# Two moves in one chain of layers: the third group's normalisation behind four query and key splits on VectorE, and the values' convolution of two groups ahead of sums and triangles on TensorE

## The chip, the cores and the metric

The kernel runs on one core of a Trainium2 chip. The metric is the device time of one execution in microseconds (us). The core has TensorE (PE, the matmuls), VectorE (DVE), ScalarE (ACT), GpSimd (POOL) and SyncE (SP, which only issues DMAs here). Each engine works through its own list of instructions in the order written; they meet only at semaphores.

## What is computed

Two layers on `x` of 2 x 1024 tokens with 128 features, with a layer normalisation behind each of four parts. Only the first and the third part matter here:

```python
x = _layernorm(x + _L0_attn_ref(x, ...))   # softmax attention, 8 heads
x = _layernorm(x + _L0_ffn_ref(x, ...))    # gated network, 512 hidden
x = _layernorm(x + _L1_attn_ref(x, ...))   # delta rule, 4 heads, chunks of 32
x = _layernorm(x + _L1_ffn_ref(x, ...))

# in _L0_attn_ref
xn = (x - mu) * rsqrt(var + eps) * gamma + beta
q, k, v = xn @ Wq + bq, xn @ Wk + bk, xn @ Wv + bv
p = softmax(q @ k.T / sqrt(dk))

# in _L1_attn_ref
q = silu(causal_dwconv(x @ Wq, conv_q))    # the same for k and v
q, k = l2norm(q), l2norm(k)
A = kb @ k.T                               # per head and chunk of 32
T = inv(eye + tril(A, -1))
```

## The kernel before, in words

The order of work is written out by hand: one program per engine, with a semaphore wait wherever one engine needs another's result. The tokens are cut into four groups of 512 (`GROUPS`, numbered 0 to 3 here; "the third group" is group 2).

**The first stage** makes the queries, keys and values of the first attention. For a group `g`, DVE takes statistics (`x_stats(g)`), POOL raises them to the power -0.5 (`x_rstd(g)`, line 903), and DVE writes the normalised rows (`normalise_x(g)`, line 1199, four instructions of 128x128). PE transposes them (`xn_transposes(g)`, line 1751), ACT copies them out with gamma and beta (`load_xnT(g)`, line 660), and PE multiplies with the three weights (`project_q`, `project_k`, `project_v`, lines 1760, 1767, 1780). Queries and keys are wanted in two parts: ACT writes the leading one (`leading_q`, `leading_k`, lines 666 and 670), and DVE the rest (`rest_q`, `rest_k`, lines 1205 and 1210). SP stores both parts to scratch in DRAM (lines 385 to 392), first of all the 32 rows that heads 0 and 1 need, of groups 0 and 1, in eight DMAs; when all eight have landed (`first_rows_stored`), SP and ACT load head 0's stacks `qst` and `kst` (lines 409, 410, 683, 684). PE's first row scores (`row_scores`, lines 1806 and 1807) wait for these, and DVE takes the row maxima (`row_max`, line 1245). On PE the row scores stand behind `project_v(2)`, and that group's own products behind `project_v(1)`, which waits for `values(0)` on DVE (line 1222). `values(0)` waits for `bv_spread`, a copy that ACT makes right behind `load_xnT(2)` (line 681). After that come 32 half heads of scores, exponentials (line 703) and products, each with a small transfer of its negated row maxima into the stack (`load_shift`, line 415).

**The third stage**, about 349 to 412 us into the span, makes the queries, keys and values of the delta rule. For each group PE does three convolutions, `conv(g, i)` with `i` 0 for the keys, 1 for the queries and 2 for the values (12 matmuls each, lines 1679 to 1681), the gates (`gate_products`, line 1689), the transposes of the next group's input (`transposes`, line 1664), the sums of squares of keys and queries (`sums(g, 0)` and `sums(g, 1)`, line 1699), and for the group before it the values' and keys' transposes (`v_to_tokens`, line 1710, `k_to_tokens`, line 1720) and the products within chunks (`triangles`, 256 small matmuls, line 1740). ACT applies silu to each convolution (line 730), copies the transposes (`vtok_copy`, line 635, `ktok_copy`, line 639), loads the next group's input (`load_x`, lines 620 and 622), and then changes its table, takes the gates' exponentials and the inverse norms (`norms`, lines 629 and 631), and changes the table back. DVE splits the loaded input (`split_x`, line 1129), squares (`square`, line 1137), scales by the norms (`normalise`, line 1142), makes the gates' logits (lines 1150 to 1160) and masks the triangles (lines 1179 and 1180). In group 0 it also finishes the normalisation of the layer before (`normalise_rows2(3)`, line 1103), while POOL prepares filters (lines 1023 to 1027). The keys' and the values' convolution of one group use the same bank, so the second waits for the silu of the first. Behind this stage stand the inverses of the triangles, one batch on POOL and one on DVE (`invert`, lines 549 and 551), a long row of filter matmuls (line 1917), the recurrence and the last network.

The list of PE in the third stage, which the change edits:

```python
for g in range(GROUPS - 1):
    conv(g, 0)
    gate_products(g)
    ...
    transposes(g + 1)
    conv(g, 1)
    ...
    if g >= 1:
        v_to_tokens(g - 1)
    sums(g, 0)
    if g >= 1:
        triangles(g - 1)
    conv(g, 2)
    if g >= 1:
        k_to_tokens(g - 1)
    sums(g, 1)
```

Of the kernel before, what the change touches and what calls it, by code (L numbers as in the profile page):

```python
# [56 lines left out]
def program(nc, dr, out_dram, x_dram, q_scratch, k_scratch, ctx):  # L57
# [201 lines left out]
    def nth_conv(g, i):  # L259
        return 3 * g + KQV_ORDER[g].index(i) + 1  # L260

    def nth_norm(g, i):
        return 2 * g + (i if g < GROUPS - 1 else 1 - i) + 1
# [3 lines left out]
    with nc.Block() as block:  # L267
# [818 lines left out]
        def _(dve):  # L1086
# [97 lines left out]
            def x_stats(g):  # L1184
                dve.wait_ge(x_in[g], 16)
                for n in range(4):
                    last = nc.vector.bn_stats(st6[:, g, n, :], X[:, 4 * g + n, :])
                link(last)
                for n in range(4):
                    last = nc.vector.bn_aggr(mv[:, g, n, :], st6[:, g, n, :])  # L1190
                link(last)
                nc.vector.tensor_scalar(rs[:, g, :], mv[:, g, :, 1], LN_EPS, None, ALU.add).then_inc(x_stats_ready, 1)

            def normalise_x(g):
                dve.wait_ge(x_rstd_ready, g + 1)
                if g >= 2:
                    dve.wait_ge(xnT_psum, g - 1)
                for n in range(4):
                    last = nc.vector.tensor_scalar(xn[:, g % 2, n, :], X[:, 4 * g + n, :], mv[:, g, n, 0:1],
                                                   rs[:, g, n:n + 1], ALU.subtract, ALU.mult)  # L1200
                last.then_inc(xn_ready, 1)

            def rest_q(g):
                dve.wait_ge(q_hi, g + 1)
                nc.vector.scalar_tensor_tensor(qsp[g][:, 1, :], ps[:, Q_BANK[g], :], bq[:, 0:1], qsp[g][:, 0, :].bitcast(F32),
                                               ALU.add, ALU.subtract).then_inc(q_lo, 1)

            def rest_k(g):
                dve.wait_ge(k_hi, g + 1)
                nc.vector.scalar_tensor_tensor(ksp[g][:, 1, :], ps[:, K_BANK[g], :], bk[:, 0:1], ksp[g][:, 0, :].bitcast(F32),  # L1210
                                               ALU.add, ALU.subtract).then_inc(k_lo, 1)
# [3 lines left out]
            normalise_x(0)  # L1215
            normalise_x(1)
            x_stats(2)
            normalise_x(2)
            def values(g):
                b, half = g // 2, g % 2  # L1220
                dve.wait_ge(v_psum, g + 1)
                nc.vector.tensor_tensor(vp[:, 8 * b:8 * b + 8, 4 * half:4 * half + 4, 0:DK0],
                                        ps[:, V_BANK, :].rearrange("p (t h e) -> p h t e", t=4, e=DK0),
                                        bv_all[:].rearrange("p (h o e) -> p h o e", o=1, e=DK0).broadcast_to([P, 8, 4, DK0]), ALU.add).then_inc(v_ready, 1)
# [3 lines left out]
            rest_k(0)  # L1228
            rest_q(1)
            rest_k(1)  # L1230
            x_stats(3)
            dve.wait_ge(bv_spread, 1)
            values(0)
# [351 lines left out]
        def _(pe):  # L1585
# [58 lines left out]
            def y_product(g):  # L1644
                pe.wait_ge(lo2_ready, 12 * g + 12)
                for k in range(FB):
                    last = product3(ps[:, 7, :], weights(W3 + D * k, D), (h2_hi[:, 2, k, :], h2_lo[:, 2, k, :]), k == 0, k == FB - 1)
                last.then_inc(y2_psum, 1)
# [18 lines left out]
            def conv(g, i):  # L1667

                if i != 1 and i == KQV_ORDER[g][0] and g >= 1:
                    pe.wait_ge(silu_done, 3 * g)  # L1670
                if i == 1 and g >= 1:
                    pe.wait_ge(ln_done, 2 * g)
                if i == KQV_ORDER[g][2]:
                    pe.wait_ge(silu_done, 3 * g + 1)
                bank = ps[:, (1, 2, 1)[i], :]
                for t in range(CONV):
                    cols = slice(GT * (g % 2) + t, GT * (g % 2) + t + GT)
                    xh, xl = x_hi[:, g // 2, cols], x_lo[:, g // 2, cols]
                    nc.tensor.matmul(bank, wc_lo[:, i, t, :], xh, start=(t == 0), stop=False)  # L1679
                    nc.tensor.matmul(bank, wc_hi[:, i, t, :], xl, start=False, stop=False)  # L1680
                    last = nc.tensor.matmul(bank, wc_hi[:, i, t, :], xh, start=False, stop=(t == CONV - 1))
                last.then_inc(conv_psum, 1)

            def gate_products(g):
                pe.wait_ge(xf_ready, g + 1)
                if g >= 1:
                    pe.wait_ge(ln_done, 2 * g - 1)
                for n in range(4):
                    last = nc.tensor.matmul(ps[:, 3, 20 * n:20 * n + 20], xf[:, P * n:P * n + P], wgates[:], start=True, stop=True)
                last.then_inc(gates_psum, 1)  # L1690

            def sums(g, i):

                pe.wait_ge(sq_ready, nth_norm(g, i))
                if i == 0:
                    pe.wait_ge(gates_biased, g + 1)
                else:
                    pe.wait_ge(silu_done, 3 * g + 2)
                nc.tensor.matmul(ps[:, (3, 2)[i], :], head_ones[:], sq[:, i, :], start=True, stop=True).then_inc(ss_psum, 1)

            def v_to_tokens(g):
                pe.wait_ge(silu_done, nth_conv(g, 2))
                for loaded in (xf_ready, xhi_ready, xlo_ready):
                    pe.wait_ge(loaded, min(g + 3, GROUPS))
                if g == GROUPS - 1:
                    pe.wait_ge(ktok_ready, g)
                for n in range(4):
                    t = 4 * g + n
                    off = FIRL - 1 + P * (t % 8)
                    last = nc.tensor.transpose(ps[:, 0, P * n:P * n + P], vpad[:, t // 8, off:off + P], ident[:])  # L1710
                last.then_inc(vtok_psum, 1)
# [216 lines left out]
            for g in range(GROUPS - 1):  # L1928
                pe.wait_ge(xhi_ready, g + 1)
                pe.wait_ge(xlo_ready, g + 1)  # L1930
                conv(g, 0)
                gate_products(g)
                if g == 0:
                    y_product(GROUPS - 1)
                transposes(g + 1)
                conv(g, 1)
                if g == 0:
                    y2_to_tokens(GROUPS - 1)
                if g >= 1:
                    v_to_tokens(g - 1)  # L1940
                sums(g, 0)
                if g >= 1:
                    triangles(g - 1)
                conv(g, 2)
                if g >= 1:
                    k_to_tokens(g - 1)
                sums(g, 1)
# [297 lines left out]
```

## Time and profile before

| what | before |
|---|---|
| median of 3 runs | 593.5 us (591.52 to 593.85) |
| the profiled execution, its own time | 589.53 us |
| its span in the trace | 587.8 us |
| PE busy | 545.9 us, 93% |
| DVE busy | 398.1 us, 68% |
| ACT busy | 325.6 us, 55% |
| POOL busy | 178.7 us, 30% |
| mean granted TensorE clock | 0.988 |

Times of an instruction are its start from the span's beginning and its duration. "Busy" leaves out waiting. The chain of waits is the row of pieces that ended last, followed back from the last instruction; what isn't on it costs nothing as long as it stays off it. A granted clock of 1.00 is 2.4 GHz, 0.50 is 1.2 GHz.

### The profile page before, as it was taken

To read this page: it belongs to the slowest core of one execution; us is meant where nothing else is said; L and a number is where in the kernel's file an instruction comes from. 1 tells how busy PE (TensorE), PEld (TensorE's weight loads), DVE (VectorE), ACT (ScalarE), POOL (GpSimd) and SP (SyncE) were. 2 spreads that over 40 slices of the span, in tenths; PEclk is the share of its full clock that TensorE was granted. 3 is DMA by queue.
4 is the path that set the end of the run, shared out by engine and by line. 5 is a ranking of instruction groups with operands and counts; after the bars stand their busy time and mean duration, and the time that the engine had idled before them with its cause. 6 is when DMAs were issued, how large, how long until landed. Compare 5 with 4: busy or idle time off the path is not lost.

```text
span 587.8 us, 17528 instructions
## 1 busy us (share of the span) xinstructions
PE 545.9 (93%) x7486; PEld 372.9 (63%) x7486; DVE 398.1 (68%) x766; ACT 325.6 (55%) x575; POOL 178.7 (30%) x343
## 2 busy tenths in 40 slices
PE   3699999999999999999999999799999789989995
PEld 2445555555555556777778787577566677667774
DVE  5697999998999945354452534444889961379685
ACT  2317888788888885656556554367832430125441
POOL 7100111353554433010010103428987225010202
PEclk9899999999999999999999999899999989999998
DMA  4688756555332000001000000012374300000001
GB/s 121 140 233 211 211 130 148 108 124 97 73 58 57 3 4 2 0 1 38 1 1 1 1 1 0 10 29 44 61 127 103 75 4 3 5 3 1 0 20 54
DMA packets 54227, 33.82 MB, mean 58 GB/s; under 512 B 39029, under 2 KB 45685, under 8 KB 54150
## 3 DMA queue, kind: packets, MB, share of 16 engines
q1 hardware_dynamic: 48998, 31.65, 24.0%
q10 hardware_dynamic: 5152, 1.05, 1.1%
q8 instruction: 59, 0.97, 0.7%
q14 instruction: 18, 0.15, 0.1%
HBM read 20.83 MB, written 9.44 MB: 51 GB/s over the span
## 4 chain that ended last, share of the span: by engine, by line
PE 68%; DVE 12%; DMA 8%; ACT 6%; issue 3%; SPq 1%; POOL 1%; POOLq 0%; ACTq 0%; DVEq 0%
PE ps L1842 10%; PE ps L1827 9%; PE ps L1589 7%; PE ps L1590 7%; PE ps L1591 7%; DMA qst<-shift_sb 5%; PE ps L2027 3%; DVE inv_flat L549 3%; PE ps L2159 3%; PE ps L1806 3%; PE ps L2160 3%; DVE inv_flat L551 2%; ACT prob L703 2%; PE ps L2019 2%; PE ps L1679 1%
## 5 line engine op out<-in xcount | busy, mean ns | idle before, releaser
L1245 DVE TENSOR_REDUCE nmx<-ps 128x1 f32<-128x1024 f32 x128 | 154.1, 1217 | 16.5 <-PE ps L1807 15.2
L703 ACT ACTIVATE prob<-ps 128x512 f32<-128x512 f32 x256 | 137.5, 597 | 26.3 <-PE ps L1827 26.0
L1842 PE MATMUL ps<-prob,vp 128*32 128x128 f32 x2048 | 78.9, 278 | 0.0
L1827 PE MATMUL ps<-qst,kst 50*128 50x512 f32 x256 | 73.5, 492 | 4.5 <-ACT prob L703 3.4
L1842 PEld LDWEIGHTS ps<-prob,vp 128*32 128x32 f32 x2048 | 49.1, 109 | 39.7 <-ACT prob L703 22.7
L1118 DVE TENSOR_TENSOR h_lo<-hf,h_hi 128x512 fp32r<-128x512 f32 x48 | 33.1, 689 | 52.4 <-ACT h_hi L607 50.2
L1589 PE MATMUL ps<-h_hi,w_lo 128*128 128x512 f32 x144 | 57.9, 402 | 2.4 <-DVE h_lo L1118 2.4
L1590 PE MATMUL ps<-h_lo,w_hi 128*128 128x512 f32 x144 | 57.0, 396 | 0.0
L1591 PE MATMUL ps<-h_hi,w_hi 128*128 128x512 f32 x144 | 56.9, 395 | 0.0
L1806 PE MATMUL ps<-kst,qst 48*128 48x512 f32 x128 | 52.7, 413 | 2.3 <-DMA kst<-k_scratch 1.7
L1807 PE MATMUL ps<-kst,qst 48*128 48x512 f32 x128 | 51.4, 403 | 0.0
L1827 PEld LDWEIGHTS ps<-qst,kst 50*128 50x128 f32 x256 | 29.3, 183 | 34.5 <-ACT prob L703 22.9
L606 ACT ACTIVATE hf<-ps,ffn_scale 128x512 f32<-128x512 f32 x32 | 22.1, 691 | 34.3 <-PE ps L1591 32.7
L885 POOL TENSOR_SCALAR rs<-mv 128x4 f32<-128x4 f32 x8 | 3.0, 376 | 122.4 <-DVE mv L1096 122.3
L924 POOL CAST nsplit<-nmx 128x4 fp32r<-128x4 f32 x32 | 6.0, 188 | 105.3 <-DVE nmx L1245 103.0
L1917 PE MATMUL ps<-vpad,fir_diag 32*32 32x512 f32 x1088 | 36.7, 597 | 0.1
L1589 PEld LDWEIGHTS ps<-h_hi,w_lo 128*128 128x128 f32 x144 | 27.0, 188 | 11.8 <-issue 4.0
L1591 PEld LDWEIGHTS ps<-h_hi,w_hi 128*128 128x128 f32 x144 | 27.0, 188 | 6.5
L1590 PEld LDWEIGHTS ps<-h_lo,w_hi 128*128 128x128 f32 x144 | 27.1, 188 | 6.0
L837 ACT ACTIVATE h_hi<-ps 128x512 fp32r<-128x512 f32 x32 | 17.7, 601 | 22.4 <-PE ps L2160 19.8
L1917 PEld LDWEIGHTS ps<-vpad,fir_diag 32*32 32x32 f32 x1088 | 21.3, 103 | 13.2 <-issue 6.3
L1806 PEld LDWEIGHTS ps<-kst,qst 48*128 48x128 f32 x128 | 23.7, 185 | 6.4 <-DVE nmx L1245 3.7
(262 smaller groups left out, 1101.5 us busy)
## 6 DMA issues: line engine op xcount, KB each, us to landing
qst<-q_scratch SPq DMA_DIRECT2D x31, 192.0 KB, 4.5
kst<-k_scratch SPq DMA_DIRECT2D x31, 192.0 KB, 5.0
w_raw<-L_ffn_h_w SPq DMA_DIRECT2D x8, 256.0 KB, 3.9
kd<-ka SPq DMA_DIRECT2D x8, 256.0 KB, 6.0
X<-L_attn_x SPq DMA_DIRECT2D x4, 256.0 KB, 5.3
qst<-shift_sb SPq DMA_DIRECT2D x64, 4.0 KB
q_scratch<-w_hi SPq DMA_DIRECT2D x2, 512.0 KB, 5.2
k_scratch<-w_lo SPq DMA_DIRECT2D x2, 512.0 KB, 3.2
```

Source lines behind the costliest of these rows:

```text
L606: nc.scalar.activation(hf[:, o, :], bank, ACT.Gelu, scale=scale)
L703: nc.scalar.activation(prob[:, n % PROBS, GT * (t % 2):GT * (t % 2) + GT], ps[:, RINGB + i % RING, :], ACT.Exp, scale=SCORE_SCALE).then_in ...
L1118: nc.vector.tensor_tensor(h2_lo[:, layer, o, :], hf[:, o, :], h2_hi[:, layer, o, :].bitcast(F32), ALU.subtract).then_inc(lo2_ready, 1)
L1245: nc.vector.tensor_reduce(nmx[:, u % 2, j:j + 1], pair, AX.X, ALU.max, negate=True).then_inc(max_done, 1)
L1589: nc.tensor.matmul(out, wl, xh, start=start, stop=False)
L1590: nc.tensor.matmul(out, wh, xl, start=False, stop=False)
L1591: return nc.tensor.matmul(out, wh, xh, start=False, stop=stop)
L1806: nc.tensor.matmul(ps[:, bank, :], qst[0:48, p, P * k:P * k + P], kst[0:48, p, 0:GT], start=True, stop=True)
L1807: nc.tensor.matmul(ps[:, bank + 1, :], qst[64:112, p, P * k:P * k + P], kst[64:112, p, GT:S], start=True, stop=True).then_inc(max_psum, 1)
L1827: nc.tensor.matmul(ps[:, RINGB + i % RING, :], kst[r:r + 50, p, P * t:P * t + P], half_of(qst[r:r + 50, p, :], u % 2), start=True, stop=Tr ...
L1842: last = nc.tensor.matmul(ps[32 * j:32 * j + 32, PVB, P * half:P * half + P], vp[:, h, t, :], prob[:, n % PROBS, c:c + P], start=(t == 0), ...
L1917: last = nc.tensor.matmul(ps[32 * g:32 * g + 32, FIR_BANK[k] + h, :], fir_diag[f, (0, FIRL)[k] + t, :], vpad[f, g // 2, off:off + GT], sta ...
```

## The change

Nothing is added or removed. On DVE the four instructions of `normalise_x(2)` move behind `rest_q(0)`, `rest_k(0)`, `rest_q(1)` and `rest_k(1)`, ahead of `x_stats(3)`. On PE `conv(g, 2)` of groups 0 and 1 moves ahead of `sums(g, 0)` (and for group 1 of `triangles(0)` too); of group 2 it stays where it is.

```diff
@@ DVE, first stage
             normalise_x(0)
             normalise_x(1)
             x_stats(2)
-            normalise_x(2)
...
             dve.wait_ge(qk_bias_in, 2 * 16)
             rest_q(0)
             rest_k(0)
             rest_q(1)
             rest_k(1)
+            normalise_x(2)
             x_stats(3)
             dve.wait_ge(bv_spread, 1)
             values(0)
@@ PE, third stage
                 if g >= 1:
                     v_to_tokens(g - 1)
+                if g < 2:
+                    conv(g, 2)
                 sums(g, 0)
                 if g >= 1:
                     triangles(g - 1)
-                conv(g, 2)
+                if g == 2:
+                    conv(g, 2)
                 if g >= 1:
                     k_to_tokens(g - 1)
                 sums(g, 1)
```

The order on DVE in the first stage, as a difference. Names in brackets are semaphores; `rstd_ready` is POOL's power, `q_hi` and `k_hi` are the leading parts from ACT.

```order
-L1199 TENSOR_SCALAR xn<-X,mv,rs 128x128 [waits xnT_psum,rstd_ready]
-L1199 TENSOR_SCALAR xn<-X,mv,rs 128x128 x3
 L1205 SCALAR_TENSOR_TENSOR qsp<-ps,bq,qsp 128x512 [waits q_hi,qk_bias_in]
 L1210 SCALAR_TENSOR_TENSOR ksp<-ps,bk,ksp 128x512 [waits k_hi]
 L1205 SCALAR_TENSOR_TENSOR qsp<-ps,bq,qsp 128x512 [waits q_hi]
 L1210 SCALAR_TENSOR_TENSOR ksp<-ps,bk,ksp 128x512 [waits k_hi]
+L1199 TENSOR_SCALAR xn<-X,mv,rs 128x128 [waits xnT_psum,rstd_ready]
+L1199 TENSOR_SCALAR xn<-X,mv,rs 128x128 x3
```

The four rests no longer stand behind the normalisation and its wait for POOL.

The order on PE in the third stage, group 1, before. Semaphores of the first stage are used again here, so the names in brackets are old ones: `stats_ready` is that a square is ready, `bv_spread` that the gates' logits are, `bv_summed` counts the silus. L1710 is `v_to_tokens(0)`, L1699 `sums`, L1740 `triangles(0)`, L1679 the first matmul of a convolution, L1720 `k_to_tokens(0)`.

```order
L1710 MATMUL ps<-ident,vpad 128x128 [waits wv_in,qk_bias_in,qk_weights_in,bv_summed]
L1710 MATMUL ps<-ident,vpad 128x128 x3
L1699 MATMUL ps<-sq,head_ones 128x512 [waits bv_spread,stats_ready]
L1740 MATMUL ps<-kq 32x64 [waits xnT_ready]
L1740 MATMUL ps<-kq 32x64 x63
L1679 MATMUL ps<-x_hi,wc_parts 128x512 [waits bv_summed]
...
L1720 MATMUL ps<-ident,kq 128x128 [waits q_psum,xnT_ready]
```

The same place of the changed kernel, where every line number is one higher:

```order
L1711 MATMUL ps<-ident,vpad 128x128 [waits wv_in,qk_bias_in,qk_weights_in,bv_summed]
L1711 MATMUL ps<-ident,vpad 128x128 x3
L1680 MATMUL ps<-x_hi,wc_parts 128x512 [waits bv_summed]
...
L1700 MATMUL ps<-sq,head_ones 128x512 [waits bv_spread,stats_ready]
L1741 MATMUL ps<-kq 32x64 [waits xnT_ready]
L1741 MATMUL ps<-kq 32x64 x63
L1721 MATMUL ps<-ident,kq 128x128 [waits q_psum,xnT_ready]
```

The twelve matmuls of the values' convolution now stand between the transposes and the wait for the square.

## Rows read from the trace of the kernel before

**Rows 1.** The page, the chain that ended last, shares by line.

```profile
PE ps L1842 10%; PE ps L1827 9%; PE ps L1589 7%; PE ps L1590 7%; PE ps L1591 7%; DMA qst<-shift_sb 5%; PE ps L2027 3%; DVE inv_flat L549 3%; PE ps L2159 3%; PE ps L1806 3%; PE ps L2160 3%; DVE inv_flat L551 2%; ACT prob L703 2%; PE ps L2019 2%; PE ps L1679 1%
```

**Rows 2.** The chain in order of time (start, duration, what), first stage and attention.

```profile
16.85 0.35 SPq L385
...
20.05 2.02 DMA k_scratch<-ksp
...
22.50 5.75 DMA kst<-k_scratch
...
28.92 1.23 DVE nmx L1245
...
44.84 5.56 DMA qst<-shift_sb
...
112.78 4.07 DMA qst<-shift_sb
```

**Rows 3.** Timeline, first stage: start, duration, engine, line, operation [idle before <-releaser].

```profile
13.27 0.69 ACT L666 ACTIVATE qsp<-ps,bq 128x512 fp32r<-128x512 f32 x1 [1.17 <-PE ps L1760]
13.45 2.71 DVE L1199 TENSOR_SCALAR xn<-X,mv,rs 128x128 f32<-128x128 f32 x4 [1.49 <-POOL rs L903]
...
16.26 0.69 ACT L670 ACTIVATE ksp<-ps,bk 128x512 fp32r<-128x512 f32 x1 [0.17 <-PE ps L1767]
...
17.45 0.66 PE L1751 MATMUL ps<-ident,xn 128*128 128x128 f32 x4
...
18.07 0.73 DVE L1210 SCALAR_TENSOR_TENSOR ksp<-ps,bk,ksp 128x512 fp32r<-128x512 f32 x1
...
18.83 0.25 ACT L681 COPY bv_all<-ps 128x128 f32<-128x128 f32 x1
...
20.11 0.69 DVE L1222 TENSOR_TENSOR vp<-ps,bv_all 128x512 f32<-128x512 f32 x1
...
20.85 2.08 PE L1780 MATMUL ps<-wv_sum,xnT 128*128 128x128 f32 x8 [2.74 <-DVE vp L1222]
...
25.63 1.06 PE L1780 MATMUL ps<-wv_sum,xnT 128*128 128x128 f32 x8
```

**Rows 4.** Stretches: bounds, length, busy of PE, PEld, DVE, ACT, POOL, PEclk, DMA.

```profile
22.00:23.00 1.00, 1.00 (x6) 1.00 (x5) 0.47 (x3) 0.00 (x0) 0.00 (x0) 0.50 0.00 0
...
370.50:374.60 4.10, 0.84 (x5) 0.42 (x4) 3.95 (x16) 1.20 (x3) 0.94 (x3) 1.00 0.00 0
374.60:377.60 3.00, 2.94 (x131) 2.00 (x131) 0.61 (x2) 0.00 (x0) 0.00 (x0) 0.70 0.02 5
```

**Rows 5.** The chain in order of time, third stage, groups 0 and 1.

```profile
359.20 0.86 PE ps L1699 x2
...
362.89 0.60 ACT vpad L730
...
370.55 0.69 DVE x_lo L1129
...
373.94 0.68 DVE sq L1137
...
377.62 0.73 PE ps L1679
...
381.40 0.47 ACT vpad L730
...
381.89 0.58 ACT ka L639
```

**Rows 6.** Timeline, third stage: POOL and DVE side by side, and triangles of group 2.

```profile
368.14 2.38 POOL L1023 TENSOR_TENSOR fir_diag<-eye,fir_l 128x992 f32<-128x992 f32 x1
...
370.82 0.62 POOL L1027 TENSOR_SCALAR wo<-wo,rmsw 128x128 f32<-128x128 f32 x1
...
371.15 1.11 DVE L1103 TENSOR_SCALAR X<-X,mv,rs 128x128 f32<-128x128 f32 x4
...
404.50 1.48 PE L1740 MATMUL ps<-kq 32*32 32x64 f32 x128
```

## The prediction

> **What bounds the kernel now.** I read the page first. Its chain of waits is spread over all stages [rows 1]: the attention's matmuls, the gated network's, the inverses on DVE, the last network. No engine bounds everything, so an edit pays only where the chain passes it. I then read the chain in order of time around both edits, the timeline there for the instructions that the chain leaves out, and the busy time of short stretches for the clock.
>
> In the first stage the chain runs from DVE to SP [rows 2]: the first store of a split query starts at 16.85, eight stores follow one another, the last one lands at 22.07, the loads of head 0's stacks land at 28.25, and only then does DVE take its first row maximum (28.92). The reader is to see what stands ahead of 16.85. The leading part of group 0's queries was ready at 13.27 + 0.69 = 13.96 [rows 3], and DVE could have made the rest then, but it was at 13.45 inside `normalise_x(2)`, which took 2.71 us.
>
> In the third stage the chain passes PE's `sums(0, 0)`, then ACT's silu of the values at 362.89, a long run of ACT, the split of the input at 370.55 and the square of group 1 at 373.94, `sums(1, 0)` right behind it, and only at 377.62 the values' convolution of group 1 [rows 5]. Between 370.50 and 374.60 PE is busy for 0.84 us of 4.10, and in the next 3.00 us its granted clock is 0.70, that is, partly at 1.2 GHz; before it fell PE had idled for 3.3 of those 4.1 us, waiting for the split and the square [rows 4]. The convolution needed nothing of what it stood behind.
>
> **The change, part one: the third group's normalisation.** The four rests now follow ACT. `rest_q(0)` can start at 14.0 in place of 16.1. `rest_k(1)` waits for the leading part that ACT ends at 16.26 + 0.69 = 16.95, so with its 0.73 us it ends at 17.7 in place of 18.8 [rows 3]. On SP the first store goes out at 14.8; eight issues of some 0.46 us each would be through by 18.4, but the last two need `rest_k(1)`: they go out at 17.9 and 18.3, where the last went out at 20.05 [rows 2]. The stacks' loads start 1.7 us earlier on SP. Of head 0's four loads two are issued by ACT, behind the copy of `bv_spread`, and that gets later, as follows.
>
> The moved normalisation starts at 17.75 and takes 1.11 us, the price of the same four instructions where POOL is mostly done [rows 6]; it ends at 18.9. PE's transposes of that group start then in place of 17.45. From their start to the end of the bias copy ACT and PE took 18.83 + 0.25 - 17.45 = 1.63 us [rows 3], so that copy ends at 20.6 in place of 19.08. `values(0)` started at 20.11, held by the statistics of the fourth group on DVE; these took the 1.3 us between 18.80 and 20.11 and end at 20.2 now, so the copy becomes its release: 20.65 to 21.35. `project_v(1)` starts at about 21.45 in place of 20.85. PE's block from there to the end of `project_v(2)` took 25.63 + 1.06 - 20.85 = 5.84 us, over half of it at 1.2 GHz [rows 3, 4], and ends at 27.3. ACT's loads go out at 20.7 and 21.1 in place of the 22.09 and 22.50 that released the chain, and land at 21.1 + 5.75 = 26.85. The row scores start with the later of the two, at 27.3; before, they started just behind the landing at 28.25, some half a microsecond ahead of the row maximum at 28.92 [rows 2], at 28.4. That is a gain of 1.1 us. Bounds: 0, if the loads land no earlier, since they share the queues with what follows; 1.6, if PE keeps its 2.4 GHz through the shorter idle (1.9 us in place of 2.74, broken by the transposes) and the landing is what ends last. I take 1.1, the sum of the rows as they stand. From the first row maximum on, DVE and PE are busy one behind the other, so it passes on.
>
> **Part two: the values' convolution.** Group 0: `sums(0, 0)` costs the chain 0.86 us between the transposes and the convolution [rows 5]. The convolution moves ahead of it, and its silu starts at 362.0 in place of 362.89. Both sums are done by 362.86 + 0.86 = 363.7 as before, before ACT reads them, so they are now hidden beside ACT's table load. ACT runs without an outside wait from there to the copies that feed the split of group 2's input; the split starts at 369.7 in place of 370.55. PE ends `conv(1, 1)` at 370.5 as before, since its total work is unchanged.
>
> Group 1: the values' transposes start at 370.55, the convolution at 371.0, and at full clock it takes 362.89 - 360.06 = 2.83 us [rows 5], so it ends at 373.8. The square ended at 373.94 + 0.68 = 374.62; 0.86 earlier it ends at 373.76. So the convolution fills the wait exactly, PE has next to no idle time, and the clock should stay at 2.4 GHz. Then `sums(1, 0)` 0.86, `triangles(0)` 1.41 to 1.48, the price of the same 128 recorded matmuls in group 2 at full clock [rows 6], and `k_to_tokens(0)` 0.66, as four transposes took at 17.45 [rows 3]: ACT's copy of the keys starts at 376.8 in place of 381.89. That is 5.1 us, made of 0.86 of `sums(0, 0)`, some 2.8 of the convolution that moved into the idle time, and some 1.4 that the same work took longer at 1.2 GHz (377.62 to 381.40 for the convolution alone, against 2.83 [rows 5]). ACT's table load follows that copy in both orders, and from there each wait is relative: the same pieces at the same distances, up to the inverses on DVE.
>
> Against this stands one contact that is new. `normalise_rows2(3)` follows the split on DVE and ran at 371.15, when POOL had 0.3 us left of its last filter instruction [rows 6]. It now starts at 370.4, beside the end of the first and the whole of the last two of POOL's three. The nearest row is `normalise_x(2)` at 13.45, the same kind of instruction beside POOL's head sums: 2.71 us for four that cost 1.11 elsewhere, 1.6 us too long [rows 3]. POOL is through at 371.44 here, so at most 371.44 - 370.4 = 1.0 us of standing still can come, and none at least; square, sums and all behind would be that much later. I take 0.4, since the four instructions can slip in between POOL's, as the fact that 13.45's four did not wait for all of POOL's work suggests. The Trainium skill (SBUF — State Buffer, section "Who interferes with whom") states that a DVE instruction in a two-port mode and GpSimd exclude each other for a whole instruction, whoever comes second waiting; by that rule the delay is nearer 1.0 than 0.4, and it speaks against this half of the change. The row at 13.45 agrees with it.
>
> Part two gives 5.1 - 0.4 = 4.7 us, with 3.6 and 5.2 as ends.
>
> **The sum.** 1.1 + 4.7 = 5.8 us. The profiled execution took 589.53 us, so the changed one would take 583.7. The median of the runs lies 4.0 us above that execution (593.5), so the forecast of the median is 593.5 - 5.8 = **587.7 us**.
>
> **The rivals.**
> *The start gives nothing.* The loads are limited by what the queues move, or PE's block gets later than I sum. For it: PE's block ends within 0.5 us of the landing. Against it: the first store is 2 us earlier and SP issued without a gap. Only part two stays: 593.5 - 4.7 = 588.8.
> *POOL and DVE collide in full.* By the row at 13.45 the four instructions lose 1.6 us, and POOL's own end is pushed back with them: part two gives 5.2 - 1.6 = 3.6, the whole 4.7, the time 588.8. By the skill's rule named above this is the case to expect wherever both run; the trace so far has it at one place out of the two that I looked at.
> *The gain of part two is eaten later.* Behind the third stage stand two inverses on two engines, some 25 us of filter matmuls and transfers. If one of them is held by something that did not move, the rest waits for it. Against it: all of them start from results of this stage. I price it at half of part two: 593.5 - 1.1 - 2.3 = 590.1, and up to 592.
> *Slower: the attention falls into another phase.* The shift transfers stand on the chain in six places, with landings from 4.07 to 5.56 us [rows 2]. A shift may land late when the large loads of later stacks are under way. The start of scores moves by 1.1 us against transfers that move by 1.7. If all six took the longest landing in place of about 4.3, this adds up to 7 us, and 593.5 - 5.8 + 7 = 594.7. It decides from an added landing of about 1 us at every place. Against it: every load of the attention waits for a score or an exponential, so the transfers move along. That the change doesn't do what it says is ruled out by the two orders shown ahead.
>
> **How the numbers follow.** The forecast gets 0.60, the start without gain 0.14, the full collision 0.12, the eaten gain 0.10, the slower case 0.04. The forecast's own range is 586.0 to 589.0. Runs of the kernel before differ by 2.3 us among three, so the range of 8 in 10 reaches from 585.3 to 591.0: it takes in the two rivals at 588.8 and half of the eaten case. About 0.5%, 3 us, is what a measurement can tell from no change. Faster by more means below 590.5: 0.60 + 0.14 + 0.12 and a little of the eaten case, less some for the spread of runs, 0.87. Within 0.5%: 0.10. Slower: 0.03.
>
> **What would show it.** In the profile of the changed kernel: the first store's issue near 14.8, the last of the eight near 18.3, the first row maximum at 27.8 or so; granted clock between 21 and 24 us tells which end part one has. In the third stage: the values' silu of group 0 near 362.0 less what part one gave; no idle time of PE over 0.7 us ahead of `sums(1, 0)`; a granted clock of 1.00 through group 1; `normalise_rows2(3)` between 1.1 and 2.1 us long; the keys' copy 4.7 us closer to the start of the stage. The forecast is wrong if PE still idles 2 us ahead of that sum, if DVE's squares get later than the convolution's end by over 1 us, or if the distance from the keys' copy to the end has grown.

## The result and the profile after

| | median of the runs, us | lowest to highest | runs | profiled execution, its span, us |
|---|---|---|---|---|
| kernel before | 592.51 | 588.71 to 593.85 | 4 (the three shown ahead and a fourth, 588.71) | 589.53, 587.8 |
| changed kernel | 584.21 | 583.73 to 584.70 | 4 | 584.60, 582.8 |

The ratio is 0.987, with a 95% interval of 0.9821 to 0.992: the kernel became faster, by more than was forecast. 584.2 lies 3.5 us below the forecast of 587.7 and 1.1 us below the low end of its range (585.3). Between the two profiled executions the difference is 4.9 us, and the interval reaches from 4.7 to 10.6 us, so the first question is how large the gain is at all. A few runs of nearly every kernel are over 1.5% longer than its fastest one; medians and ranges here include them, the ratios leave them out.

**The page.** The groups that stood at the head of the chain are still there, with lines one to four further down in the code [rows 1]. From the page of the changed kernel:

```profile
span 582.8 us, 17528 instructions
PE 546.2 (94%) x7486; PEld 372.8 (64%) x7486; DVE 395.0 (68%) x766; ACT 325.5 (56%) x575; POOL 177.9 (31%) x343
PEclk9799999999999999999999999999999889999998
PE 76%; DVE 12%; ACT 5%; DMA 4%; issue 2%; SPq 1%; POOL 0%; POOLq 0%; DVEq 0%; ACTq 0%
```

**First stage.** The timeline of the changed kernel (start, duration, engine, line, operation, and in brackets the idle time before and its releaser), to be held against [rows 3]:

```profile
14.57 0.35 SPq L385 DMA_DIRECT2D q_scratch<-qsp  x1
...
16.21 0.75 DVE L1210 SCALAR_TENSOR_TENSOR ksp<-ps,bk,ksp 128x512 fp32r<-128x512 f32 x1
...
16.88 1.11 DVE L1199 TENSOR_SCALAR xn<-X,mv,rs 128x128 f32<-128x128 f32 x4
...
17.79 0.43 SPq L392 DMA_DIRECT2D k_scratch<-ksp  x1
...
19.42 0.26 ACT L681 COPY bv_all<-ps 128x128 f32<-128x128 f32 x1
...
20.22 0.45 ACTq L684 DMA_DIRECT2D kst<-k_scratch  x1
20.45 1.78 PEld L1781 LDWEIGHTS ps<-wv_sum,xnT 128*128 128x128 f32 x8 [1.99 <-DVE vp L1222]
20.45 2.08 PE L1781 MATMUL ps<-wv_sum,xnT 128*128 128x128 f32 x8 [1.75 <-DVE vp L1222]
...
27.39 0.50 PE L1807 MATMUL ps<-kst,qst 48*128 48x512 f32 x1
...
27.93 1.22 DVE L1246 TENSOR_REDUCE nmx<-ps 128x1 f32<-128x1024 f32 x1 [0.48 <-PE ps L1808]
```

The stores go out 2.3 us earlier, the moved normalisation takes 1.11 us in place of 2.71, and the first row maximum comes at 27.93 in place of 28.92 [rows 2]. What held the row scores is no longer the landing of the stacks: PE runs without a pause from 20.45 to them, at 1.2 GHz for most of that time. The busy time of three stretches of the changed kernel (bounds, length, PE, PEld, DVE, ACT, POOL, granted clock, DMA share, GB/s):

```profile
17.00:21.00 4.00, 1.21 (x6) 0.97 (x7) 3.50 (x16) 0.93 (x2) 1.01 (x1) 0.80 0.59 134
21.00:25.00 4.00, 4.00 (x12) 2.45 (x11) 1.32 (x5) 0.69 (x1) 0.00 (x0) 0.50 1.01 238
25.00:27.00 2.00, 2.00 (x12) 1.38 (x11) 1.04 (x2) 1.02 (x2) 0.00 (x0) 0.70 1.01 170
```

A granted clock of 0.80 over 4 us means 4 x 0.20 x 2 = 1.6 us at half clock; with the other two that makes 1.6 + 4.0 + 1.2 = 6.8 us. The clock fell between 19.30 and 19.40, over a microsecond before PE had work again (20.45):

```profile
17.00:19.30 2.30, 0.66 (x4) 0.42 (x4) 2.23 (x13) 0.56 (x1) 0.00 (x0) 1.00 0.86 200
19.40:20.40 1.00, 0.00 (x0) 0.00 (x0) 0.69 (x1) 0.27 (x2) 0.94 (x1) 0.50 0.00 0
```

In the 2.3 us before the fall PE had been busy for 0.66, the group's transposes. In the kernel before it fell at 20.8, as PE's block began (20.85), and stayed down for 3.4 us. The two profiles differ earlier too, where their code is the same. The first product of the keys, in the kernel before and in the changed one:

```profile
12.96 1.54 PE L1767 MATMUL ps<-xnT,wk 128*128 128x512 f32 x2
12.72 1.02 PE L1768 MATMUL ps<-xnT,wk 128*128 128x512 f32 x2
```

At 12.7 us PE was already at its quick pace in the changed kernel, and in the first profile only at about 14.0. That isn't work of the edit, and it comes up again below.

**Third stage.** The timeline of the changed kernel around group 1:

```profile
368.40 0.69 DVE L1129 TENSOR_TENSOR x_lo<-ps,x_hi 128x512 fp32r<-128x512 f32 x1 [3.42 <-ACT x_hi L622]
...
369.00 0.62 POOL L1027 TENSOR_SCALAR wo<-wo,rmsw 128x128 f32<-128x128 f32 x1
369.00 1.20 DVE L1103 TENSOR_SCALAR X<-X,mv,rs 128x128 f32<-128x128 f32 x4
...
371.87 1.28 DVE L1137 TENSOR_TENSOR sq<-kq 128x512 f32<-128x512 f32 x2
...
372.28 0.39 PE L1682 MATMUL ps<-x_hi,wc_parts 128*128 128x512 f32 x1
...
372.61 1.12 PE L1700 MATMUL ps<-sq,head_ones 128*128 128x512 f32 x2
372.71 0.60 ACT L730 ACTIVATE vpad<-ps 128x512 f32<-128x512 f32 x1 [2.22 <-PE ps L1682]
373.67 1.48 PE L1741 MATMUL ps<-kq 32*32 32x64 f32 x128
...
375.82 0.58 ACT L639 COPY ka<-ps 128x512 f32<-128x512 f32 x1 [2.51 <-PE ps L1721]
```

and the stretch around it:

```profile
370.00:376.00 6.00, 6.00 (x147) 4.07 (x146) 3.80 (x14) 1.27 (x3) 0.00 (x0) 1.00 0.01 3
```

The last matmul of the values' convolution (372.28) runs into the sums of the squares (372.61): PE is busy for all 6 us, and the granted clock is 1.00 where it was 0.70 [rows 4]. The keys' copy starts at 375.82 in place of 381.89 [rows 5], 6.07 us earlier. Of these 1.29 had been gained before this stage (its first input split starts that much earlier); 4.78 are gained in it.

**Behind it.** The end moved by 4.9 us, not by 6.07. The chain of the changed kernel in order of time (start, duration, what), at the second inverse:

```profile
415.77 0.51 SPq L494
416.28 0.04 issue
416.32 3.89 DMA low_dram<-low
420.21 0.02 issue
420.23 3.88 DMA inv_flat<-low_dram
424.11 0.02 issue
424.13 0.22 DVE inv_flat L549
```

and of the kernel before:

```profile
421.75 0.51 SPq L494
422.26 0.04 issue
422.30 1.91 DMA low_dram<-low
424.21 0.02 issue
424.22 3.72 DMA inv_flat<-low_dram
427.94 0.02 issue
427.97 0.67 DVE inv_flat L549
```

The store leaves 5.98 us earlier, but lands after 3.89 us in place of 1.91; the inverse starts only 3.84 us earlier. Behind it PE ran at half clock twice near 460 and 467 (3.4 us each), where before it did so once, near 471.

### The profile page after: what moved, and what is told of

It reads as the page before. It is cut to its first block, busy times and chain, and to the rows that moved or that the text cites. A ratio compares the mean times of both kernels' runs of the same rounds, so it can differ in the third digit from the quotient of the medians.

```text
span 582.8 us, 17528 instructions
## 1 busy us (share of the span) xinstructions
PE 546.2 (94%) x7486; PEld 372.8 (64%) x7486; DVE 395.0 (68%) x766; ACT 325.5 (56%) x575; POOL 177.9 (31%) x343
## 4 chain that ended last, share of the span: by engine, by line
PE 76%; DVE 12%; ACT 5%; DMA 4%; issue 2%; SPq 1%; POOL 0%; POOLq 0%; DVEq 0%; ACTq 0%
PE ps L1843 11%; PE ps L1828 10%; PE ps L1590 7%; PE ps L1592 7%; PE ps L1591 7%; PE ps L2031 3%; DVE inv_flat L549 3%; PE ps L1807 3%; PE ps L2163 3%; PE ps L2164 3%; DVE inv_flat L551 2%; ACT prob L703 2%; DMA qst<-shift_sb 2%; PE ps L2023 2%; PE ps L1680 2%
## 5 line engine op out<-in xcount | busy, mean ns | idle before, releaser
L1246 DVE TENSOR_REDUCE nmx<-ps 128x1 f32<-128x1024 f32 x128 | 154.0, 1217 | 14.7 <-PE ps L1808 13.4
L1918 PEld LDWEIGHTS ps<-vpad,fir_diag 32*32 32x32 f32 x1088 | 21.0, 103 | 13.5 <-issue 6.6
L2163 PE MATMUL ps<-h_lo,wc_parts 128*128 128x512 f32 x64 | 26.8, 419 | 0.9 <-DVE h_lo L1472 0.9
```

The costliest lines, as they stand in the source:

```text
L1246: nc.vector.tensor_reduce(nmx[:, u % 2, j:j + 1], pair, AX.X, ALU.max, negate=True).then_inc(max_done, 1)
L1918: last = nc.tensor.matmul(ps[32 * g:32 * g + 32, FIR_BANK[k] + h, :], fir_diag[f, (0, FIRL)[k] + t, :], vpad[f, g // 2, off:off + GT], sta ...
L2163: nc.tensor.matmul(ps[:, 4 + o, :], w, h_lo[:, 0, k, :], start=(k == 0), stop=False)
```

## The experiments

Eleven experiments ran, with nine different kernels, on three chips: 1 to 4 on the first, 5 to 8 on the second, 9 to 11 on the third. On each the kernel before ran beside them: medians 589.78 (32 runs), 589.82 (26) and 589.4 (17). Numbers of lines in brackets below are those of the kernel before, unless said otherwise.

**1. The kernel before, unchanged.** No edit.

> The kernel before, unchanged, to see how far its executions lie apart. Theory A (the forecast's sum of 6 us holds, and the other 2 to 3 us of the measured 8.3 are the spread of the kernel before): its runs scatter again over 588 to 594 us, and this profile differs from the first at a place that can be named, a cold stretch of TensorE or a late landing. Theory B (the sum is too small by 2 us in a typical run, and the first profile of the kernel before was untypically quick): nearly all runs lie at 591 to 594 and the profile shows where 2 to 4 us more go than in the first one.

Measured: 590.36 us (588.78 to 594.31, 12 runs), ratio 1.0006 (0.9981 to 1.003). With the runs beside it there are 87 of this kernel, with the median 589.8; 11 of them took 593.5 us or more. So the profiled execution of 589.53 us was a typical one, and the median of three from which the forecast started (593.5) was a high one: theory A. At a rate of 11 in 87, two of three runs at 593.5 or more come about once in 20 times. Chance is therefore the likely reason, not a shown one; on which chip the first comparison ran is not on record.

**2. The start alone.**

```
             x_stats(2)
-            normalise_x(2)
...
             rest_k(1)
+            normalise_x(2)
             x_stats(3)
```

> Only the third group's normalisation is moved. Forecast's theory: 1.1 us faster (0 to 1.6), first row maximum about 27.9 us into the span. Rival: nothing at all at the end, as the attention settles to its own pace. If the first stage is where the kernel before scatters, this kernel's runs lie closer together and its median gains more than 1.1 us.

Measured: 590.56 us (587.55 to 592.8, 12 runs), ratio 1.0001 (0.9974 to 1.0027). No gain shows in the times; the interval leaves room for 1.5 us, so it decides neither for the forecast nor for its rival. In this profile the first row maximum stood at 28.03, where experiment 1 had it too. What its run shows besides is the price of group 1's wait. The stretch 368 to 382, in experiment 1 and in experiment 2 (columns as above):

```profile
368.00:382.00 14.00, 10.68 (x162) 7.05 (x161) 5.97 (x19) 4.24 (x9) 5.80 (x12) 0.88 0.07 10
```

```profile
368.00:382.00 14.00, 10.68 (x159) 7.28 (x158) 5.85 (x18) 3.10 (x6) 5.33 (x11) 0.76 0.06 11
```

14 x 0.24 x 2 = 6.7 us at half clock against 14 x 0.12 x 2 = 3.4, with the same order of instructions and the same idle time on PE. From the split of group 2's input [L1129] to the gates of group 1 [L1167] this execution took 14.83 us, against 13.63 in the first profile and 13.67 in experiment 1.

**3. The convolutions alone.** Groups 0 and 1, the start as before.

```
+                if g < 2:
+                    conv(g, 2)
                 sums(g, 0)
...
-                conv(g, 2)
+                if not (g < 2):
+                    conv(g, 2)
```

> Only the values' convolution of groups 0 and 1 is moved. Forecast's theory: 4.7 us faster (3.6 to 5.2), no idle time of PE over 0.7 us ahead of the sum of group 1. Theory B puts the missing 2 us here: 6 to 7 us faster in the median, since the idle stretch that goes costs more at 1.2 GHz in most runs than in the one profiled.

Measured: 586.03 us (584.87 to 594.74, 9 runs), ratio 0.9928 (0.9898 to 0.9958), that is 4.2 us with the interval 2.5 to 6.0. No half clock in group 1, and PE doesn't idle ahead of `sums(1, 0)`; from L1129 to L1167 10.16 us. The interval holds the forecast of 4.7 and leaves out theory B's 6 to 7.

**4. The changed kernel again.**

> Both moves, again. If the parts add up, its gain is that of the two kernels with one part each, and lies between 5 and 8.5 us; its runs stay within 1.5 us of each other as in the first measurement.

Measured: 585.88 us (582.91 to 595.04, 12 runs), ratio 0.9918 (0.9883 to 0.9953): 4.8 us against the kernel before on the same chip. From the split to the gates 9.67 us, first row maximum at 27.50. Two things expected here did not come: the gain is just under the 5 to 8.5 us, and the runs don't lie within 1.5 us of each other.

**5. Group 1's convolution alone.**

```
+                if g == 1:
+                    conv(g, 2)
                 sums(g, 0)
...
-                conv(g, 2)
+                if not (g == 1):
+                    conv(g, 2)
```

> Of the three moves only the values' convolution of group 1 goes ahead; group 0 and the first stage are as before. Theory: the square of group 1 is ready 0.86 us later than with both groups moved, so PE idles about 0.8 us behind the convolution; from the split of group 2's input on DVE (the start of L1129) to the gates' sigmoids of group 1 (L1167) the distance of 13.6 us shrinks by 3.9 us, and no stretch of group 1 runs at 1.2 GHz. Rival: the distance shrinks by all 4.8 us, and group 0's move is worth nothing. In the median 3 to 4 us faster than before.

Measured: 585.54 us (584.17 to 589.42, 9 runs), ratio 0.9933 (0.9911 to 0.9956). From L1129 to L1167 9.57 us, 4.06 fewer than before, at a granted clock of 1.00. The 0.8 us of idle time that I expected behind the convolution isn't there: PE started the convolution at 372.76 and was busy until the sums at 375.66. One instruction block in one iteration carries nearly all of what part two gains.

**6. Only the clock.** The kernel before, with eight matmuls ahead of `sums(1, 0)` whose results nothing reads, in a bank that is free there.

```
+                if g == 1:
+                    for _ in range(8):
+                        nc.tensor.matmul(ps[:, 7, :], wc_hi[:, 0, 0, :], x_hi[:, 0, 0:GT], start=True, stop=True)
                 sums(g, 0)
```

> The kernel before with eight extra matmuls (results unused) in the idle time of PE ahead of the sum of group 1: only the clock is kept, no work is moved. Theory: the clock's share of part two is 1.4 us when the stretch at 1.2 GHz is 3.4 us long and more when it is 6.8 us long, so the distance from L1129 of group 2's input to L1167 of group 1 shrinks by 1.2 to 1.6 us against the first profile, and the median by 1 to 2 us. Rival: the clock is a bystander, nothing changes, and all of part two is the work moved into the idle time.

Measured: 587.87 us (585.25 to 599.58, 12 runs), ratio 0.997 (0.9948 to 0.9992), that is 1.8 us with the interval 0.5 to 3.1. The convolution still stands behind the sums; only the waiting time is filled. The timeline of this kernel, and its stretch:

```profile
373.77 1.29 DVE L1137 TENSOR_TENSOR sq<-kq 128x512 f32<-128x512 f32 x2
374.51 1.12 PE L1699 MATMUL ps<-sq,head_ones 128*128 128x512 f32 x2 [0.79 <-DVE sq L1137]
375.57 1.48 PE L1740 MATMUL ps<-kq 32*32 32x64 f32 x128
376.97 0.50 PE L1679 MATMUL ps<-x_hi,wc_parts 128*128 128x512 f32 x1
```

```profile
368.00:382.00 14.00, 12.53 (x176) 8.97 (x175) 6.51 (x20) 5.43 (x9) 6.99 (x14) 1.00 0.09 15
```

In experiment 2 the same sums took 2.08 us and the triangles 1.89 on the chain, both at half clock; here the timeline has 1.12 and 1.48. From L1129 to L1167 it is 12.47 us, 1.16 fewer than before. So the filled wait is worth 1.2 us at one half-clock stretch of 3.4 us, 2.4 at one of 6.8, and the moved work makes the rest of the 4.06.

**7. A filled wait in the first stage.** The changed kernel, with eight matmuls without a reader ahead of `project_v(1)`.

```
+            pe.wait_ge(q_hi, 1)
+            pe.wait_ge(k_hi, 1)
+            for _ in range(8):
+                nc.tensor.matmul(ps[:, 5, :], ksp[0][:, 0, 0:P], qsp[0][:, 0, :], start=True, stop=True)
             project_v(1)
```

> The changed kernel with eight extra matmuls (results unused) in PE's idle time between the third group's transposes and project_v(1). Theory: in the changed kernel PE's block at 1.2 GHz, not the landing of head 0's stacks, is what the first row scores wait for; with the clock kept the block ends 1.5 us earlier, the landing decides, and the first row maximum comes at 26.6 to 27.2 us in place of 27.5 to 27.9. Rival: the landing is as late as the block, nothing is gained, or the fill itself delays project_v(1). Median 0 to 1 us below that of the changed kernel.

Measured: 582.6 us (581.43 to 584.25, 6 runs), ratio 0.9881 (0.9857 to 0.9905). The timeline of its PE, with its own line numbers (L1796 is the fill, L1781 `project_v`, L1811 the row scores):

```profile
18.71 2.08 PE L1796 MATMUL ps<-qsp,ksp 128*128 128x512 f32 x8
20.71 1.16 PE L1781 MATMUL ps<-wv_sum,xnT 128*128 128x128 f32 x8
...
26.50 0.46 PE L1811 MATMUL ps<-kst,qst 48*128 48x512 f32 x1 [1.58 <-DMA kst<-k_scratch]
```

and its stretch:

```profile
16.00:28.00 12.00, 9.13 (x50) 6.16 (x48) 8.44 (x24) 3.41 (x6) 1.01 (x1) 1.00 0.86 181
```

The eight matmuls of `project_v(1)` take 1.16 us in place of 2.08, PE is through by 24.9, and the landing of the stacks ends last: the row maximum moves to 27.03, 0.9 us ahead of the changed kernel's first profile. The median lies 2.3 us below the 584.9 of all runs of the changed kernel, more than the 0 to 1 us expected, but no run of the changed kernel stood beside it on this chip.

**8. All three convolutions ahead of the sums.**

```
-                if g < 2:
+                if True:
                     conv(g, 2)
...
-                if g == 2:
+                if not (True):
                     conv(g, 2)
```

> The changed kernel with group 2's values' convolution moved ahead as well. Theory: PE idles only 0.84 us there, so the move hides at most that; the triangles of group 1 come some 2 us later and with them POOL's inverse, while the keys' copy on ACT stays within 0.5 us of where it was: same time as the changed kernel, or up to 1 us slower. Rival: the 4 us gain of group 1 repeats itself, 2 us or more faster.

Measured: 584.95 us (582.43 to 589.18, 12 runs), ratio 0.9927 (0.9905 to 0.9949). That is no gain over the changed kernel in the times, as expected. In the trace group 2's distance from the split [L1129] to the gates [L1167] is 9.51 us against 9.76 in the changed kernel's first profile, so 0.25 us and not 4.

**9. The same with a longer fill near the end.** Experiment 7, and nineteen filling matmuls in place of the eight that the kernel already issues ahead of `times_inverse(1)`.

```
-            keep_busy(7, 8)
+            keep_busy(7, 19)
```

> The changed kernel with the eight extra matmuls in the first stage and, behind the first batch's state inputs, 19 idle-time matmuls in place of 8, so that PE has next to no idle time ahead of the second batch's times_inverse (L1988 in the changed kernel), which took 5.50 us at 1.2 GHz against 3.95 us at full clock. Theory: the half-clock stretch goes, the 128 recorded matmuls take 3.95 us, and the median is 1 to 1.5 us below that of the kernel with the first fill alone. Rival: the added 11 matmuls (some 2.4 us at full clock) outlast the landing of the inverse and cost what they save: no difference.

Measured: 585.35 us (580.64 to 591.73, 12 runs), ratio 0.9907 (0.987 to 0.9943). Its profile shows no half clock there (1.00 from 455 to 475), but the times gain nothing: on the same chip the shorter fill had 583.81 (experiment 10). The fill ends at 465.15 and `times_inverse(1)` starts at 465.07, where the shorter fill let it start at 464.25 in experiment 10. Against that delay of 0.8 us stand 1.55 where the 128 recorded matmuls take 5.50 us, at half clock for the most part (experiment 4), and next to nothing where they take 4.14 or 3.95 without the longer fill (experiments 10 and 11). The half clock that this fill was to remove isn't there in every execution.

**10. Experiment 7 again.** Same kernel.

> The changed kernel with the eight extra matmuls in the first stage alone, again, beside the changed kernel on the same chip. Theory: 0.3 to 1.5 us below the changed kernel in the median; the first row maximum at 27.0 against 27.5 to 27.9 us. Rival: the 3 us between the two medians measured on two chips so far were chance, no difference.

Measured: 583.81 us (582.03 to 585.16, 6 runs), ratio 0.9898 (0.9857 to 0.994), first row maximum at 27.17, granted clock 1.00 in the first stage. That is 0.7 us below the changed kernel on the same chip (experiment 11).

**11. The changed kernel, a third time.**

> The changed kernel a third time, on the same chip as the two fills. By the forecast's sum, taken from the kernel before's own median of all runs (589.8 us), 584.0 us; by the first ratio (0.987) 582.1; by the second (0.9918) 585.0.

Measured: 584.51 us (581.32 to 597.64, 6 runs), ratio 0.9894 (0.985 to 0.9938). All 22 runs of the changed kernel have the median 584.9, the 12 of experiments 7 and 10 have 583.3. The fill of the first stage is the best version that ran, but the intervals overlap, and experiment 9, which has the same fill, had 585.35: a gain of 0.7 to 1.6 us over the changed kernel is likely and not settled. Experiment 11 itself fell between the 584.0 of the forecast's sum and the 585.0 of the second ratio.

## Why the prediction was wrong, and where it was right

Four places of the program separate the terms. The traces give, in us (the row maximum and the start of the third stage, the third of the four instructions of group 3's statistics [L1096], as starts; the others as distances):

| execution | first row maximum | start of third stage | from there to group 1's gates | from the gates to the end |
|---|---|---|---|---|
| before | 28.92 | 361.51 | 22.67 | 203.6 |
| experiment 1 (before) | 28.03 | 360.82 | 22.70 | 203.5 |
| experiment 2 (start alone) | 28.03 | 360.46 | 23.87 | 203.9 |
| experiment 3 (convolutions alone) | 28.88 | 361.66 | 18.34 | 204.0 |
| changed kernel | 27.93 | 360.22 | 17.89 | 204.7 |
| experiment 4 (changed kernel) | 27.50 | 359.96 | 17.85 | 205.7 |
| experiment 11 (changed kernel) | 27.64 | 360.02 | 18.15 | 201.4 |

**The terms of the sum were right, part one in the traces alone.** Part one was forecast at 1.1 us. The five executions with the start as before (the first profile and experiments 1, 3, 5, 6) have their first row maximum at 28.82 on average, the five with the moved normalisation (changed kernel, 2, 4, 8, 11) at 27.75: 1.1 us. At the start of the third stage the same two sets are 1.5 us apart. The medians of experiments 1 and 2 do not show this part.

In the changed kernel's first profile the number came out by two errors of a microsecond that cancelled. I had left ACT's leading part of the keys at 16.26 [rows 3]; it came at 15.49, since PE had reached its quick pace earlier in this execution, so the bias copy ended at 19.68 and not 20.6, and PE's block began at 20.45 and not 21.45. And the block took 26.40 + 1.06 - 20.45 = 7.0 us, not the 5.84 of before, with 6.8 us at half clock where the first profile had 3.4. Where PE reached that pace as late as in the first profile, in experiments 2, 4 and 8, the steps came as forecast:

| | forecast | exp. 2 | exp. 4 | exp. 8 |
|---|---|---|---|---|
| first store goes out | 14.8 | 14.54 | 15.02 | 15.00 |
| last of the eight goes out | 18.3 | 18.29 | 18.42 | 18.52 |
| bias copy ends | 20.6 | 20.47 | 20.59 | 20.69 |
| PE's block begins | 21.45 | 21.25 | 21.37 | 21.47 |
| PE's block ends | 27.3 | 27.07 | 27.03 | 27.19 |
| stacks land (ACT's second load) | 26.85 | 27.35 | 26.77 | 26.68 |
| row scores start | 27.3 | 27.49 | 26.96 | 27.12 |

In experiments 4 and 8 PE's block ended last, as forecast, in experiment 2 the landing.

So the size of part one depends on that draw. With the late pace the row maximum stands at 29.01 (the first profile, 3, 5, 6) against 27.73 (2, 4, 8): 1.3 us. With the early pace it is 28.03 (experiment 1) against 27.79 (changed kernel, 11): 0.2 us, from three executions only. With the half clock filled away it is 27.03 on average (7, 9, 10), so the half clock costs the changed order some 0.7 us.

Part two was forecast at 4.7 us and measured 4.78 at the keys' copy; by the table's third column it is 4.8 in the changed kernel and experiment 4, 4.5 in experiment 11 and 4.3 in experiment 3, against the mean of 22.67 and 22.70. Of its own terms, the 0.86 of `sums(0, 0)` came out exactly (values' silu 360.74 against 362.89: 2.15 = 1.29 + 0.86), the clock 1.2 us at one stretch of 3.4 us (experiment 6) against 1.4, the convolution 2.9 (experiment 5 less experiment 6) against 2.8. The forecast gives part two's whole once as 5.1 and once as 5.2, and its bounds add up to 586.7 to 589.9, not to 586.0 to 589.0; nothing hangs on either.

**The contact on DVE was over-priced.** I took 0.4 us for `normalise_rows2(3)` beside POOL, with 0 and 1.0 as bounds. It took 1.20 us against 1.11: 0.1, and the same 1.20 or 1.21 in all eight profiles with group 0's convolution moved. It did run beside the end of one filter instruction (368.67 + 0.35) and all of the last (369.00, 0.62). POOL was through at 369.62, so by the rule of the Trainium skill (SBUF — State Buffer, section "Who interferes with whom") the first of the four should have been held until then, some 0.6 us; it took 0.44 in place of 0.34, and the POOL instruction its usual 0.62. Here the measurement speaks against the rule for these pieces. So does the first profile: the first of the four started at 371.15 and took 0.37 us, though the same POOL instruction ran from 370.82 to 371.44. The four at 13.45 had agreed with it: they took 1.28, 0.76, 0.57 and 0.33 us, and the first three ended within 0.1 us of the POOL instruction beside them. Why one pair collides and the other doesn't is left open.

**The step that failed is the last one: the base.** "The median of the runs lies 4.0 us above that execution (593.5), so the forecast of the median is 593.5 - 5.8." The sum from the profiled execution, 583.7, was 0.5 us from the 584.2 measured in four runs. I then added the whole distance between the median of three runs and that execution, as if it were an overhead that every run has. It was not: with 87 runs the median of the kernel before is 589.8, and 11 of 87 lie at or above 593.5. From 589.8 the same sum gives 584.0, against 584.9 measured over 22 runs. For the same reason the gain of the first comparison, 8.3 us between medians, is too large. The ratios of experiments 4 and 11 stand for 4.8 us (2.8 to 6.9) and 6.2 us (3.7 to 8.8) of 589.8; the two medians over all runs lie 4.9 us apart, as do the two profiled executions. The sum of 5.8 is within both intervals, and up to a microsecond above these differences.

**Where that microsecond can go.** "The gain of part two is eaten later" was priced at half of part two, with the inverses held by something that did not move. Nothing of the kind holds them: in experiments 4 and 11 the inverse on DVE starts at 421.63 and 421.74, 6.3 and 6.2 us earlier than before. In the first profile the store of 3.89 us took 2.0 us of it and part was regained; in the others that store was not late. What differs from execution to execution is the last column of the table. It is 201.4 where the trace has no half clock behind the gates but in its last 5 us (experiment 11; 201.4 in experiment 6, 201.7 in 10), 203.4 to 203.9 with one stretch of 3.4 us (experiment 5 has the 203.4), 203.5 to 205.7 with 6.8 us in all (experiment 7 has the 203.5), and 208.5 in experiment 8, whose trace has 25 x 0.27 x 2 = 13.5 us of it between 500 and 525:

```profile
500.00:525.00 25.00, 23.84 (x605) 17.75 (x604) 13.06 (x43) 4.54 (x10) 1.29 (x2) 0.73 0.02 4
```

The changed kernel drew both the shortest and the two next to the longest of these tails, so the missing microsecond is of the size of this spread. Nothing on record says that the new order makes such stretches more frequent. The time at half clock of a whole run, 2 x (1 - mean granted clock) x span, is 17.5 us on average over 83 runs of the kernel before and 13.4 over 20 of the changed kernel, the runs that the ratios use; the 4 us between them are about what group 1's stretch had (3.4 or 6.8). The sign by which the forecast said it would be wrong, a longer distance from the keys' copy to the end, did appear: 207.0 us against 205.9 in the first comparison, 208.0 in experiment 4. But where no half clock fell behind the copy ahead of the last 5 us, it is 203.7 in the changed kernel (experiment 11) and 203.7 in the old order (experiment 6), so no part of the order of work shows in it. Where the microsecond went isn't shown; experiment 2, without a gain in the times, leaves room for it in part one.

**The other rivals.** The start without a gain (588.8), the full collision (588.8) and the slower attention phase (594.7) are excluded by the traces: each asked for a landmark that stayed where it was or got later. For the first of them the medians alone would not do it (experiment 2). The range failed with the base: 4.0 us lower, at 581.3 to 587.0, it holds the measured 584.2 and the 584.9 of all runs.

## What to carry to other kernels

A sum worked out from a trace belongs to the time of the traced execution; before it is carried over to a median of a few runs, ask whether the distance between them is an overhead or a draw, and put the forecast between both if it can't be told. Before two profiles are compared, look whether their clock was the same in the code that they share. On an engine that works in order, look for a wait with independent work right behind it: moving one block of 2.8 us ahead of such a wait gave 4 us, since the wait had also cost TensorE its clock. The same wait filled with idle matmuls gives only the clock's part.

## What the runs showed that was not expected

**The spread of this kernel goes with TensorE's clock.** Over the 42 runs of the kernel before on the first chip that the ratios use (experiment 1 and those beside it) the span and the mean granted clock correlate with -0.77: at 0.985 or more the mean span is 587.8 us (28 runs), between 0.978 and 0.985 589.5 (11 runs), below 592.8 (3 runs). The same program draws a different number of half-clock stretches in each execution.

**How long a short wait costs clock hung on when the fall came.** In the first stage and in group 1 the half clock lasted either 3.4 or 6.8 us. In all four stretches of 6.8 us the clock fell 0.8 to 1.4 us before PE had work again (the first stage of the changed kernel and of experiments 1 and 11; group 1 of experiment 2). In all nine of 3.4 us it fell at most 0.4 us before PE's restart, or behind it: in group 1 of the first profile at 375.8, when the sums were already running (374.66). The length of the wait doesn't sort them. In the first stage 1.75 us of waiting behind the transposes was followed by 6.8 us in the changed kernel and by 3.4 in experiments 2 and 4, with the same code; the kernel before waited 2.74 us in its first profile and had 3.4, and 3.42 us in experiment 1 and had 6.8. In that stage the start of the execution tells which it will be: of the ten profiles without a fill there, the three in which PE was at its quick pace by 12.7 us (the changed kernel's first, 1 and 11) had the clock fall at 19.1 to 19.4 and stay down for 6.8 us, the seven in which it was so by 14.0 to 15.0 had it fall at 20.8 to 21.8 for 3.4 us. A shorter wait alone did not keep the clock; work in it did (experiments 6 and 7).

**The same small store took 1.91 and 3.89 us to land** in two kernels whose code is the same there, with 2.8 and 2.9 us of issues by SP up to it. It took the longer time in the changed kernel's first profile; its cause isn't shown.
